# Embedding gathers in whole batches, and a score product placed behind a projection

## What is computed

```python
out = base_weight[input_ids]                 # 50257 x 192 table
rows = id2row[input_ids]                     # -1 where the id isn't one of 256 tuned ids
h = where(rows >= 0, train_weight[max(rows, 0)], out)
h = h + attention(layernorm(h))              # 12 heads of 16, softmax over 512 keys
h = h + switch_ffn(layernorm(h))
h = h + ttt_attention(layernorm(h))
h = h + soft_moe(layernorm(h))
```

## Time and profile before

| | us |
|---|---|
| median of 3 runs | 1441.39 (1437.11 to 1441.47) |
| the profiled execution | 1440.88 |
| its span, first to last instruction | 1439.1 |
| TensorE busy | 1285.2 (89%) |
| VectorE busy | 919.5 (64%) |
| ScalarE busy | 709.4 (49%) |
| GpSimd busy | 375.0 (26%) |
| mean granted TensorE clock | 0.957 of 2.4 GHz |

### The profile page before, as it was taken

One profiled execution on the slowest core, in us unless ns is written; L12 is line 12 of the kernel. 1 busy time (PEld: TensorE's weight loads), 2 busy tenths in 40 slices (PEclk: granted clock), 3 DMA queues, 4 the chain that ended last, 5 costly groups with the idle time before them and its releaser, 6 DMA issues. The chain is left out here.

```text
span 1439.1 us, 29210 instructions
## 1 busy us (share of the span) xinstructions
PE 1285.2 (89%) x11383; PEld 871.6 (61%) x11383; DVE 919.5 (64%) x2227; ACT 709.4 (49%) x1512; POOL 375.0 (26%) x428
## 2 busy tenths in 40 slices
PE   4789999799869999899999989898986788799999
PEld 3432333346446777577777776777764344388888
DVE  6388887412568777499888878878775787400011
ACT  1346566332124444488888865667654233343410
POOL 6400000000047776355666640000000333300000
PEclk9889999979979999899999999999997999999999
DMA  3252120100223234444343542122004000068721
GB/s 94 80 139 65 47 66 25 25 1 0 51 84 126 92 104 133 152 129 122 108 125 110 140 117 64 48 55 62 23 1 174 38 1 1 1 237 290 273 94 45
DMA packets 99285, 127.42 MB, mean 89 GB/s; under 512 B 24589, under 2 KB 87804, under 8 KB 94956
## 3 DMA queue, kind: packets, MB, share of 16 engines
q1 hardware_dynamic: 97612, 123.96, 28.1%
q0 software_dynamic: 1536, 1.59, 0.4%
HBM read 89.06 MB, written 37.88 MB: 88 GB/s over the span
## 5 line engine op out<-in xcount | busy, mean ns | idle before, releaser
L1755 POOL TENSOR_SCALAR r_grD<-gr 32x192 f32<-32x192 f32 x192 | 101.7, 529 | 101.1 <-DVE gr L1649 60.6
L723 ACT ACTIVATE PT<-bank 128x1024 f32<-128x1024 f32 x96 | 94.3, 1022 | 59.3 <-PE bank L603 58.6
L664 DVE TENSOR_REDUCE mx<-bank 128x1 f32<-128x512 f32 x176 | 109.9, 681 | 12.1 <-PE bank L586 11.8
L1486 PE MATMUL bank<-r_grD,ek 128*128 128x256 f32 x384 | 101.1, 400 | 0.0
L2481 DVE TENSOR_TENSOR eo_all<-bank,m_b2s 128x768 f32<-128x768 f32 x8 | 7.7, 957 | 142.3 <-PE bank L2442 142.3
L2473 ACT ACTIVATE x_g<-bank,m_b1s 128x128 f32<-128x128 f32 x192 | 51.4, 400 | 75.7 <-PE bank L2424 75.7
L1486 PEld LDWEIGHTS bank<-r_grD,ek 128*128 128x128 f32 x384 | 68.5, 191 | 9.5
L2357 POOL TENSOR_SCALAR m_xs<-m_xs 128x256 f32<-128x256 f32 x4 | 2.5, 631 | 263.7 <-DVE m_xs L2261 262.6
L1699 ACT ACTIVATE r_t<-r_xh,r_cd 128x64 f32<-128x64 f32 x192 | 69.9, 427 | 0.7
L1477 PEld LDWEIGHTS bank<-gr,r_A 128*128 128x128 f32 x384 | 48.4, 193 | 33.9 <-DVE gr L1649 31.7
L1321 POOL TENSOR_TENSOR rope_c<-cy,rope 128x512 f32<-128x512 f32 x48 | 60.0, 1271 | 28.3 <-DVE cy L1182 28.3
(11 more groups left out here) (369 smaller groups left out, 3211.5 us busy)
## 6 DMA issues: line engine op xcount, KB each, us to landing
wb<-in_m_w SPq DMA_DIRECT2D x32, 1152.0 KB, 6.3
k_d<-p_krows SPq DMA_DIRECT2D x48, 256.0 KB, 2.8
ek<-k_d SPq DMA_DIRECT2D x32, 384.0 KB
tgt<-c_d SPq DMA_DIRECT2D x33, 196.0 KB
c_d<-p_rows SPq DMA_DIRECT2D x32, 196.0 KB, 2.8
g_d<-gr SPq DMA_DIRECT2D x32, 192.0 KB
o_G<-g_d SPq DMA_DIRECT2D x32, 192.0 KB, 3.0
qk_d<-a_parts SPq DMA_DIRECT2D x24, 192.0 KB, 2.9
```

What stands on the lines that cost most here:

```text
L664: v.tensor_reduce(mx[u % 2][:, j // 4, j % 4:j % 4 + 1], slot(f"A{u}.{j}"), AX.X, ALU.max).then_inc(*dve.did(f"max{u}.{j}"))
L723: a.activation(PT[kt % 2][:, 2 * hp:2 * hp + 2, :], STB[s % 2][:, :, :], ACT.Exp, scale=DH ** -0.5)\
L1486: last = t_.matmul(SP_[g][:, i * B * E1:(i + 1) * B * E1], ek[r][:, p, :], grD[g][:, i, :, :].rearrange("p b e -> p (b e)"), start=False, ...
L1755: last = g_.tensor_scalar(grD[g][rr, :, b, :], b3(gr[j % RING][rr, cols(g)]), 0.0, None, ALU.bypass)
```

## The change

GpSimd gathers the base rows in whole batches: base 0, then for each b base b + 1 (all four tiles) and train b. And `AT_PE` gives "T" no product and "qk0" three: TensorE issues A0 behind qk0 of batch 3, in front of A1 and A2. TensorE's list of steps follows `AT_PE`; VectorE's order stays.

```diff
-        AT_PE = {"T": (0, 1), "qk0": (1, 3), "qk1": (3, 5), "qk2": (5, 8), "v0": (8, 11), "v1": (11, 16)}
+        AT_PE = {"T": (0, 0), "qk0": (0, 3), "qk1": (3, 5), "qk2": (5, 8), "v0": (8, 11), "v1": (11, 16)}
@@
-                def base(b, half):
-                    for t in range(b * TB + half * (TB // 2), b * TB + (half + 1) * (TB // 2)):
+                def base(b):
+                    for t in range(b * TB, (b + 1) * TB):
                         g.indirect_dma_start(out=h[:, t, :], out_offset=None, in_=ins["base_weight"],
                                              in_offset=bass.IndirectOffsetOnAxis(ap=ids_u[:, t:t + 1], axis=0)).then_inc(based[b], 16)
@@
+                base(0)
                 for b in SB:
-                    for half in range(2) if b == 0 else (1,):
-                        base(b, half)
                     if b + 1 < B:
-                        base(b + 1, 0)
+                        base(b + 1)
                     train(b)
```

## The result

The changed kernel takes 1445.81 us (median of 11 runs, 1439.75 to 1450.22) against 1437.11 us for the kernel before (11 runs, 1430.60 to 1443.59). The ratio is 1.0056, with a 95% interval of 1.0035 to 1.0077: slower by 0.56%, about 8 us. The prediction was 1442.0 us, within a range of 1432.0 to 1445.0; it was reckoned from a kernel before of 1440.88 us, so it forecast 1.1 us of loss. The profiled execution took 1447.20 us with a span of 1445.4.

What follows compares the result with a forecast made beforehand. The embedding stage was taken as one chain across engines, batch after batch, with no engine full in batches 0 and 1. Batch 0's +1.64 and A0's -0.5 gave +1.1 us on 1440.88: 1442.0 us, range 1432.0 to 1445.0.

Steps and rivals of the forecast that it cites:

- Batches 1 to 3 don't gain: GpSimd's removed idle, 2.62 us before tuned 1 and 3.54 before tuned 3, is covered by 2.0 and 11.6 us: worth nothing.
- the hold: Batch 1: ScalarE waits 5.42 us for transposes, unexplained; taken unchanged, moved by 1.64 us. Its disappearance: 1432.1 us, chance 0.18.
- My argument that it was there in each run: Batch 1's hold: timed runs at 1437.11 to 1441.47 us, none near 1431.5, so it seems present each time.
- The rival on the slower side: Batch 1: clock rises a step later, slowing passes, value products and batch 2's transposes; about 4.2 us, 1446.2, chance 0.12.
- Batch 0's +1.64: Batch 0: tuned 0 starts 1.66 us later behind two more base gathers; statistics 1.64 us late, ends +0.4 and +1.64.
- nothing of [its] own here: Batch 0: ScalarE, TensorE and SP's store queue have no work of their own and are late with the statistics.
- The rival "absorbed": Clock rises or batch 1's hold ends at the same moment; at most 0.4 us left, 1440.4 to 1440.8, chance 0.22.
- A0's -0.5: Batch 3: qk0 starts 0.88 us sooner ahead of A0; three maxima in a row, VectorE wins 0.5 us.
- Its upper end: Batch 3, A0's placing: at most 0.88 us won, the whole earlier start of qk0.
- a rise fixed to the first pass: Batches 0 and 1: TensorE's clock rises 6.9 us after the first pass and moves with the work, keeping all 1.64 us.
- one fixed in time: Clock rises stay put, so each batch halves the lateness: 1.64 to 0.82 to 0.41 us.
- the two equal delays: Batches 0 and 1: first 0.19 us weight load 6.9 us after the first pass in both; evidence against absorption.

Runs made afterwards that it cites:

- a2: The changed kernel, unchanged, traced again; one run, no ratio: batch 1's passes at 60.09 us, last maximum at 99.35 us.
- a3: The kernel before with the new gather order alone, A0 left behind batch 3's transposes; ratio 1.0071 to the kernel before.
- c3: The changed kernel with one GpSimd wait behind tuned 1 until ScalarE has copied batch 0's first projection; ratio 0.9999 to the kernel before.
- b4: The changed kernel with batch 0's gathers as before and GpSimd waiting behind tuned 2 for batch 1's transposes; ratio 0.9960 to the kernel before.
- b2: The changed kernel with the two stores of phi made to wait until tuned 0 has landed; ratio 1.0039 to the kernel before.
- d1: The changed kernel with a short GpSimd pause behind tuned 1 and phi's stores waiting for tuned 0; ratio 0.9990 to the kernel before.
- b3: The changed kernel with GpSimd waiting behind tuned 2 until TensorE has transposed batch 1, then base 3 and tuned 3; ratio 1.0007 to the kernel before.
- c4: The changed kernel with batch 0's gathers as before, a short pause behind tuned 1, then tuned 2, base 3, tuned 3; ratio 0.9984 to the kernel before.
- d2: As c4, but gathers behind the pause ordered half of base 3, tuned 2, half of base 3, tuned 3; ratio 0.9979 to the kernel before.
- c2: The changed kernel with the 12 tuned gathers of batches 1 to 3 replaced by 12 GpSimd fills; ratio 0.9969 to the kernel before.
- c1: The changed kernel with the 12 tuned gathers of batches 1 to 3 replaced by second gathers of base rows; ratio 1.0048 to the kernel before.
- a4: The kernel before with only A0 moved behind qk0 of batch 3, gathers in the old order; ratio 0.9994 to the kernel before.
- b1: The changed kernel with the 12 tuned gathers of batches 1 to 3 left out; ratio 0.9969 to the kernel before.

## Why the prediction was wrong

**The step that failed** is "*Batches 1 to 3 don't gain ... so these removals are worth nothing*", together with the hold "as it is, moved by 1.64 us". I asked of GpSimd's idle times only who waits for the rows behind them, found 2.0 and 11.6 us of cover, and priced them at nothing. The cover was real: tuned 1 to 3 were never waited for after the change. But the pauses did other work. With the 2.6 us before 33.3 batch 0's updates came on time, in all three traces of the old order, and at the 3.54 us before 54.9 the hold of the kernel before ended. Without pauses, TensorE's updates come 5 to 10 us late from batch 0's qk1 on, and that of qk2 is let go only 3.7 to 4.0 us behind the last gather, at about 57 (the changed kernel, a2, a3). One wait of 3.2 us put back into the new order (c3) takes the loss away, which shows that the missing pauses are the cause; which of them batch 0 needs is not shown, since b4 has none at 33 and is on time up to qk1. So the passes start at 59.8 to 60.1 instead of 48.1 to 53.6: 8.8 us from mean to mean of three traces each (59.9 - 51.2), less the 0.5 us of A0 8.3, against about 8 measured.

**The hold** was seen and priced for its disappearance (1432.1, chance 0.18), not for its growth. Both ends were to be had: what lasts for an unknown reason can last longer. My argument that it was there in each run, since none lay near 1431.5, was weak: with 11 runs the kernel before reached 1430.6, and its three traces have the passes of batch 1 at three places 5.5 us apart. The rival on the slower side had the right place (batch 1) and by luck nearly the right time, 1446.2 (from its own base a loss of 5.3 us, where 8 were measured), by a mechanism that didn't happen: batch 1's twelve passes took 8.74 us against 8.78 before. Its chance of 0.12 was too small for the case of a slower kernel as a whole.

**Batch 0's +1.64** was mis-sized: 3.67. GpSimd's part held, tuned 0 starting 1.64 us later against 1.66 forecast; the rest is the landing, 4.1 us against 2.1, beside the two stores of phi. The prediction said of SP's store queue that it had "nothing of [its] own here", though their issue stands in the code right behind VectorE's scaling. b2 gives the price and its cause. But it was also mis-placed: neither 3.67 nor 1.64 reached the end, b2's and d1's passes start where those of the changed kernel and c3 do. The rival "absorbed" had this (the hold ends at the same moment whatever enters it), and missed that the moment itself, the end of the gathers, moves with the change.

**A0's -0.5** was right: 16.60 us against 17.14, three maxima in 1.89 us, and 0.9994 when it stands alone, too small to be measured. Its upper end may have been too low: in the two traces where the clock fell in batch 3 without it, the stretch was 2.3 and 2.5 us longer than 16.6.

**The clock.** The rows do not bear out a rise fixed to the first pass, nor one fixed in time: TensorE's first weight load at 0.19 us comes at 42.70 in the changed kernel, 6.0 us behind the first pass at 36.67, and at 38.88 in the kernel before taken again, 5.8 us behind 33.06, against 6.9 in the earlier trace rows. Over all sixteen traces it comes 4.1 (b3) to 7.0 us (c4) behind the first pass of batch 0, between 38.0 (d2) and 44.2 us (c2), so that the two equal delays which the prediction leaned on were chance. This agrees with the rule of the Trainium skill (TensorE: Matmul & The Clock Gate, "Part 1: The HAM clock gate") that the chip's judgement has a rhythm of its own. The level in batch 0 is read from the loads, 0.34 against 0.19 us: the granted clock of the kernel before reads 1.00 from 33.0 to 39.8, where the loads take 0.34 us, and 0.50 from 53.6 to 60.4, where they take the same. Timelines of the changed kernel, then of the kernel before taken again:

```profile
41.95 0.34 PEld L197 LDWEIGHTS bank<-a_xT,a_wqk 96*128 96x128 f32 x1 [0.52 <-issue]
42.70 0.19 PEld L197 LDWEIGHTS bank<-a_xT,a_wqk 96*128 96x128 f32 x1 [0.41 <-issue]
```

```profile
38.34 0.30 PEld L197 LDWEIGHTS bank<-a_xT,a_wqk 96*128 96x128 f32 x1 [0.52 <-issue]
38.88 0.19 PEld L197 LDWEIGHTS bank<-a_xT,a_wqk 96*128 96x128 f32 x1 [0.24 <-issue]
```

## What to carry to other kernels

An engine's idle time off the critical path is not free to remove until one knows what it lets through: besides "who waits for this work" ask "what goes late while this engine never stops". Where a wait in a profile has a releaser that it calls remote, and the engine it waits for had been done for microseconds, take it for a term of the sum with both ends open and look at it in a second trace before pricing a change beside it. With gathers on GpSimd, try a gap where TensorE has to hand over to other engines, as b4 has, and see that the gathers behind it still land in time, as c4's did not.

## What the runs showed of the hardware

- While GpSimd issued indirect gathers back to back, TensorE's semaphore updates reached their waiters late, by up to 14 us by the records (b2: qk2's passes end at 42.62, the copy that waits for them starts at 57.06). The last copy held starts 3.1 to 4.6 us behind the end of the stream in b3, the changed kernel, a2, a3, b2 and c1, and 0.1 to 1.6 us behind it in the kernel before, a4 and d2; the first can start within the stream. Gathers whose rows are skipped (the changed kernel) and gathers whose rows are fetched (c1) do it alike; fills on GpSimd held nothing in c2. What couples the two engines is not shown, nor whether the profiler, which recorded every execution here, has a part in it.
- Twenty gathers in a row that ended at 37.4, 2.5 us before the first projection was copied, held nothing in batch 0 (b1). A pause of 3.2 to 3.3 us near the updates freed those behind it wholly or but for about 1 us (b4, c4, c3); pauses of 2.8 us (d1) and 1.6 us (d2) left holds of 2 to 4 us and of about 4 us.
- A gather of almost only skipped rows landed 2.1 us after its start, 4.1 us after it when 768 KB of stores were issued 0.7 us ahead of it (3.6 to 4.5 us in the eight traces with the stores in front), and again after 2.1 when they were not (b2).
- One wait of VectorE of 2.22 us in batch 3 (c4) was followed by four passes of 3.78 us instead of 1.98. From the statistics to the last maximum it was 24.8 us, against 21.1 in the changed kernel: the wait cost its own length and another 3.6 us in what followed.
